# A reciprocal on one engine replaced by a guess and a polynomial on three, and edits at both ends of a long mix

## What is computed

```python
y = (A * p + E * vt) / (A * q + E)          # per row and channel; p, q carried over time
x = x + y
comb = top-2 of softmax(xn @ gate_w.T), scattered over 8 experts
moe = sum_e comb_e * (silu(xn @ Wg_e.T) * (xn @ Wu_e.T)) @ Wd_e.T
sh  = sigmoid(xn @ wsg.T) * (silu(xn @ Sg.T) * (xn @ Su.T)) @ Sd.T
out = x + moe + sh
```

## Time and profile before

| | us |
|---|---|
| median of 3 runs (lowest, highest) | 553.49 (552.86, 554.25) |
| the profiled execution | 557.75 |
| its span | 555.6 |
| PE busy | 476.0 (86%) |
| PEld busy | 317.2 (57%) |
| DVE busy | 427.5 (77%) |
| POOL busy | 339.0 (61%) |
| ACT busy | 272.7 (49%) |
| reciprocals (L1205), 64 of them | 57.4 |

### The profile page before, as it was taken

How to read it: one execution, slowest core, us unless ns; L and a number is a source line. 1 busy time by engine, 2 the same in 40 slices (tenths; PEclk the granted TensorE clock), 3 DMA queues, 4 the chain that set the end, 5 groups by cost and what they waited for, 6 DMA issues and landing times.

```text
span 555.6 us, 11206 instructions
## 1 busy us (share of the span) xinstructions
PE 476.0 (86%) x3293; PEld 317.2 (57%) x3293; DVE 427.5 (77%) x956; ACT 272.7 (49%) x531; POOL 339.0 (61%) x419
## 2 busy tenths in 40 slices
PE   0045868999999999999999979899999999999970
PEld 0034545777677677676777757555545555555530
DVE  5989999999999999999998667576656666666650
ACT  4867466286484674865836634423333333333310
POOL 5976768648858868588584651423485565555332
PEclk9999789999999999999999989999999999999995
DMA  7971111114323314241215010425486676576453
GB/s 297 411 296 40 42 35 38 59 59 143 106 59 134 97 41 166 62 170 60 87 68 175 22 51 2 116 70 102 78 152 115 120 133 118 105 134 121 67 74 38
DMA packets 25932, 59.21 MB, mean 107 GB/s; under 512 B 6314, under 2 KB 6314, under 8 KB 24338
## 3 DMA queue, kind: packets, MB, share of 16 engines
q0 software_dynamic: 9824, 20.90, 21.0%
q1 hardware_dynamic: 16050, 37.59, 19.0%
HBM read 37.83 MB, written 20.65 MB: 105 GB/s over the span
## 4 chain that ended last, share of the span: by engine, by line
PE 37%; DVE 26%; POOL 11%; issue 10%; DMA 7%; ACT 4%; SPq 1%; another core or an unknown queue 1%; POOLq 0%; ACTq 0%; DVEq 0%
PE GU L964 13%; PE GU L1003 8%; PE DN L979 7%; DMA out<-wall,cb 5%; PE DN L1019 5%; DVE wall L1205 5%; PE XT L907 3%; DVE st L1208 2%; DVE wall L1198 2%; POOL wall L463 2%; DVE wall L1191 2%; DVE th L1318 2%; ACT wall L657 2%; DVE hx L1325 2%; DVE HS L1320 1%
## 5 line engine op out<-in xcount | busy, mean ns | idle before, releaser
L1003 PE MATMUL GU<-xt,wall 128*128 128x256 f16 x1536 | 190.9, 276 | 3.1 <-DVE xt L1230 2.4
L1003 PEld LDWEIGHTS GU<-xt,wall 128*128 128x128 f16 x1536 | 150.2, 99 | 35.1 <-DVE xt L1230 2.8
L613 POOL DMA_INDIRECT out<-wall,cb x39 | 62.0, 1590 | 81.8 <-SPq L390 36.8
L1019 PE MATMUL DN<-wall,hx 128*128 128x512 f16 x384 | 95.3, 385 | 7.2 <-DVE xb L1332 3.0
L682 ACT ACTIVATE th<-GU,scl 128x256 f32<-128x256 f32 x103 | 48.7, 473 | 95.5 <-PE GU L1003 46.0
L691 ACT ACTIVATE hx<-HS 128x256 f16<-128x256 f32 x103 | 39.2, 381 | 94.7 <-PE HS L907 55.6
L1325 DVE TENSOR_TENSOR hx<-HS,hx 128x256 f16<-128x256 f32 x103 | 42.8, 415 | 50.3 <-ACT hx L691 45.2
L1019 PEld LDWEIGHTS DN<-wall,hx 128*128 128x128 f16 x384 | 36.9, 99 | 43.9 <-issue 7.0
L964 PE MATMUL GU<-wall,kb 128*128 x240 | 61.4, 379 | 0.2 <-issue 0.2
L964 PE MATMUL GU<-wall,xnb 128*128 x228 | 58.5, 379 | 1.6 <-DVE xnb L1524 1.6
L1318 DVE SCALAR_TENSOR_TENSOR th<-th,GU 128x256 f32<-128x256 f32 x103 | 41.6, 404 | 23.7 <-ACT th L682 23.7
(11 more groups left out here) (166 smaller groups left out, 804.3 us busy)
## 6 DMA issues: line engine op xcount, KB each, us to landing
wall<-wgu SPq DMA_DIRECT2D x12, 1024.0 KB, 7.7
wall<-wd SPq DMA_DIRECT2D x12, 512.0 KB, 8.6
out<-xb SPq DMA_DIRECT2D x20, 256.0 KB
xb<-x SPq DMA_DIRECT2D x16, 256.0 KB, 2.9
cb<-ctx_t SPq DMA_DIRECT2D x16, 256.0 KB
xn_rows<-xnb SPq DMA_DIRECT2D x16, 256.0 KB
xb<-xn_rows,cb POOLq DMA_INDIRECT x39
out<-wall,cb POOLq DMA_INDIRECT x39
```

What stands on the lines that cost most here:

```text
L613: pool.indirect_dma_start(out, bass.IndirectOffsetOnAxis(ap=idsa[:, j:j + 1], axis=0), ye[j % RESULTS], None, compute_op=ALU.add).then_inc ...
L1003: ins = nc.tensor.matmul(GU[n % 2][:, g * 2 * P:(g + 1) * 2 * P], gate_up(sh_base(u // 2), wp, c)[:, f:f + P], xt_pair(n // PU * 2, xp, c) ...
L1019: ins = nc.tensor.matmul(DN[a][:], hx[n % 2][:, hp * IE + a * P:hp * IE + (a + 1) * P], down(sh_base(u // 2), wp, u % 2), start=u == 0 and ...
```

## The change

For tiles 4 to 15 the reciprocals and the product go away. ScalarE makes a first guess of 1/q from the bits of q (`guess`: an exponential of the integer pattern, 128 x 512), GpSimd multiplies denominator and numerator with it (`trial`, and copies the first column), ScalarE squares the first product twice with two shifts (`correction`), and VectorE multiplies the second product with the two quadratic factors (`divide`: 4 x 127 elements per partition, twice). Tiles 0 to 3 keep the reciprocal. `both_exps` waits for the finished quotient in place of GpSimd's product. ScalarE's high parts of an odd turn stand one place earlier.

In the ramp GpSimd waits for `add_now` of tiles 1 and 3 at two places, `shared_d_lo(0)` comes ahead of `quotient(2)`, three constants are added, and `hidden(3)` goes behind the small steps. At the other end of the mix `accumulate` comes ahead of `rows_of_lists`, the list's cast, transpose and copies come earlier (`last_expert_lo` behind them), and `earlier_adds` leaves the last expert's end out, so that an unused slot waits like a slot of the last expert.

```diff
+DIV = LAG + 1
+GUESS_SCALE, GUESS_BIAS = -math.log(2) / (1 << 23), 127 * math.log(2) + math.log(2 / 2.0614756908398154)
+DIV_SCALE = 1.0002892772687446
+DIV_BIAS, DIV_ADD = (-0.691182891301668, -1.8095403018701928), (0.9041945157263527, 0.3453715725662169)
...
-CONSTS_FIRST, CONSTS, LATE_CONSTS, WKVC = 9, 17, 2, 6
+CONSTS_FIRST, CONSTS, LATE_CONSTS, WKVC = 9, 20, 2, 6
...
+                for k, value in enumerate((GUESS_BIAS, *DIV_BIAS)):
+                    link(pool.memset(divc[:, k:k + 1], value))
...
+            def trial(t):
+                pool.wait_ge(guessed, t - DIV + 1)
+                nc.gpsimd.tensor_tensor(wkv(t, 2), wkv(t, 2), wkv(t, 0), ALU.mult).then_inc(tried, 1)
+                nc.gpsimd.tensor_tensor(wkv(t, 3), wkv(t, 3), wkv(t, 0), ALU.mult).then_inc(ymul, 1)
+
+                pool.wait_ge(ymul, t + 1)
+                nc.gpsimd.tensor_scalar(chunks(wkv(t, 3))[:, :, 0:1], chunks(part(cb, t))[:, :, 0:1], 1.0, None,
+                                        ALU.mult).then_inc(y_first, 1)
+
...
+            pool.wait_ge(nd, 2)
...
             first_product(3)
             second_product(3)
+            shared_d_lo(0)
             quotient(2)
-            shared_d_lo(0)
             norm(4, 0, agg1, norm1, k_rdy)
+            pool.wait_ge(nd, 4)
             shared_d_lo(1)
...
                 if lo_e is not None:
                     expert_lo(lo_e, 2)
+                trial(i)
                 if ws_e is not None:
                     expert_lo(ws_e, 0)
                 if i + 2 < B:
...
                 if i + 1 < B:
                     first_product(i + 1)
                     second_product(i + 1)
-                quotient(i)
                 if sq_e is not None:
                     scales(sq_e + 2, sq_e)
...
                 act.wait_ge(kp1, t + 1)
-                wait_from(act, ymul, t - 1)
+                wait_from(act, y_rdy, t - 1)
...
+
+            def guess(t):
+                act.wait_ge(nd, t + 1)
+                nc.scalar.activation(wkv(t, 0), wkv(t, 2).bitcast(I32), ACT.Exp, bias=divc[:, 0:1],
+                                     scale=GUESS_SCALE).then_inc(guessed, 1)
+
+            def correction(t):
+
+                act.wait_ge(tried, t - DIV + 1)
+                nc.scalar.activation(wkv(t, 1), wkv(t, 2), ACT.Square, bias=divc[:, 1:2],
+                                     scale=DIV_SCALE).then_inc(corrected, 1)
+                nc.scalar.activation(wkv(t, 2), wkv(t, 2), ACT.Square, bias=divc[:, 2:3],
+                                     scale=DIV_SCALE).then_inc(corrected, 1)
...
                 unit_tanh(n, 0, SHARED)
                 router_out(i - 2)
+                guess(i)
                 if i == B - 1:
...
                 act_hi(i - 1)
                 if i + 2 < B:
                     first_norm(i + 2)
+                correction(i)
                 unit_hi(n + 2, 0)
+                if hi_e is not None:
+                    expert_piece(hi_e, 0)
                 unit_tanh(n + 3, 1, SHARED)
                 if hi_e is not None:
-                    expert_piece(hi_e, 0)
+                    expert_piece(hi_e, 1)
                 if ws_e is not None:
                     expert_piece(ws_e, 4)
                 unit_hi(n + 3, 1)
                 if hi_e is not None:
-                    for k in range(1, 4):
+                    for k in range(2, 4):
                         expert_piece(hi_e, k)
                 if ws_e is not None:
...
-            shared_units(B - LAG + 2, beyond={1: [lists_t], 3: [lambda: gathered_t(0, 0)]})
+            shared_units(B - LAG + 2, beyond={0: [lists_t], 3: [lambda: gathered_t(0, 0)]})
...
+
+            def divide(t):
+                dve.wait_ge(ymul, t + 1)
+                dve.wait_ge(corrected, (t - DIV) * 2 + 2)
+                later = [grid(wkv(t, r))[:, :, 1:T] for r in range(4)]
+                STT(later[3], later[1], DIV_ADD[0], later[3], ALU.add, ALU.mult).then_inc(half_div, 1)
+                dve.wait_ge(half_div, t - DIV + 1)
+                STT(later[3], later[2], DIV_ADD[1], later[3], ALU.add, ALU.mult).then_inc(y_rdy, 1)
...
             first_stats(5)
             keys(4)
-            hidden(3, 1, SHARED)
             reciprocals(3, 2, 2)
             act_lo(2)
             small_steps(1, 0)
+            hidden(3, 1, SHARED)
...
                 if i == B - 1:
                     probabilities(0, 0, PART)
-                reciprocals(i, 0, 1)
                 hidden(n + 1, 1, SHARED)
                 if i + 1 < B:
                     keys(i + 1)
-                reciprocals(i, 1, 2)
                 hidden_lo(n + 1, 1)
-                reciprocals(i, 3, 1)
                 hidden(n + 2, 0, SHARED)
                 act_lo(i - 1)
+                divide(i)
                 small_steps(i - 2, i - 3, None if sq_e is None else sq_e + 2)
...
                 dve.wait_ge(pads_rdy, 1)
                 dve.wait_ge(rt_pos, 3)
-                wait_step(TT(cmp, cmp, r_end.unsqueeze(1).to_broadcast([P, NSLOT, E]), ALU.mult))
-                wait_step(nc.vector.tensor_reduce(r_eid, cmp, AX.X, ALU.max))
+                former = cmp[:, :, 0:E - 1]
+                wait_step(TT(former, former, r_end[:, 0:E - 1].unsqueeze(1).to_broadcast([P, NSLOT, E - 1]), ALU.mult))
+                wait_step(nc.vector.tensor_reduce(r_eid, former, AX.X, ALU.max))
...
             hidden_lo(n, 0)
             small_steps(l=B - 1)
-            rows_of_lists()
             accumulate(B - 4)
             accumulate(B - 3)
+            rows_of_lists()
             hidden(n + 1, 1, SHARED)
...
             small_steps(k=E + 1)
             hidden_lo(n - 1, 1)
-            hidden(n, 0, SHARED)
             dve.wait_ge(ids_ld, 16)
             nc.vector.tensor_copy(ids_float.unsqueeze(2), ids_back.rearrange("r (p a) -> r p a", a=LW)[:, :, 0:1]
                                   ).then_inc(ids_f, 1)
+            hidden(n, 0, SHARED)
             hidden_lo(n, 0)
-            last_expert_lo(E - 2, 0)
-            last_expert_lo(E - 2, 1)
             dve.wait_ge(ids_t, 1)
             nc.vector.tensor_copy(idsi, KT[:, 0:NSLOT]).then_inc(ids_rdy, 1)
             dve.wait_ge(pads_rdy, 1)
             TT(idsa, KT[:, 0:NSLOT], pad_of, ALU.add).then_inc(ids_rdy, 1)
+            last_expert_lo(E - 2, 0)
+            last_expert_lo(E - 2, 1)
             hidden(n + 1, 1, SHARED)
             hidden_lo(n + 1, 1)
```

7 lines of the change are left out of this document (added).

## The result

| | before | after |
|---|---|---|
| median (lowest, highest), 4 runs each | 553.87 (552.86, 554.94) | 580.72 (578.91, 584.25) |
| ratio, 95% interval | | 1.0492 (1.0455 to 1.0529) |
| the profiled execution, its span | 557.75, 555.6 | 578.91, 577.1 |
| mean granted TensorE clock in it | 0.977 | 0.973 |
| busy: PE, DVE | 476.0, 427.5 | 479.7, 401.3 |

The account below looks back on a forecast made before the run. TensorE was taken as the bound, VectorE close behind, with a chain of waits setting each turn; turns +29, lists -2.8, first gather -0.5, last add -4.9, ramp 0 make +20.8 us on 553.5: 574 us, range 556 to 587.

Parts of the forecast that it names:

- The bound and the chain: Turns: norm, trial, low part, norm, first norm, squares, factors in line; even turns 17.4 to 20.5 us, odd 19.2 to 22.7.
- The signs named ahead: Turns: VectorE idle ahead of L1244, ScalarE ahead of L664, TensorE waiting 1 to 3 us; last add 0.3 us behind rows.
- Rival (a): Whole kernel: the chain has slack, VectorE decides, TensorE runs without waits; 539.6 us, chance 0.17.
- the ring: Turns: the path of waits across engines from one start of the scans to the next, forecast at 20.5 and 22.7 us.
- Rival (b): Odd turns: later scans escape GpSimd's scale steps, 2.3 us per odd turn come back; 564 us, chance 0.12.
- Contention, 0.4 us per turn: Turns: VectorE's two-input factors stretch beside GpSimd's products; 0.4 us added per turn, 10 us more in all with 1.27.
- "+2" and "+1": Forecast extra us: +2 for turns 4 and 5 together, +1 for turns 14 and 15 together.
- By these accounts all would fit: Per tile, busy time: VectorE 2.4 us less, ScalarE 1.8 more, GpSimd 1.25 more, which by itself would fit.
- Both ends: Ramp and end of the mix: lists -2.8 us, first gather -0.5, last add -4.9, ramp 0.
- the lists: End of the mix: `accumulate` moved ahead, six products done in the shade of TensorE's wait; -2.8 us (0 to -4.3).
- The ramp at 0: Start of the kernel: gains at tile 1 and a later product of tile 2 put at 0, between -2 and +3 us.
- rival (c): Turns: TensorE's stop for the quotient in odd turns lowers its clock; +6 us, 580 us, chance 0.08.

Follow-up runs that it names:

- squares_first: The changed kernel with the two squares put ahead of the first norm on ScalarE: 565.02 us, 1.0211 of the kernel before.
- ends_only: The kernel before with `accumulate` first, the list's cast, transpose and copies earlier, and the shorter waits of unused slots: 547.3 us, ratio 0.9875.
- adds_only: The kernel before with only the shorter waits of unused slots: 549.47 us, ratio 0.9945.
- the parts alone: Three runs, each with one part of the change on the kernel before: division in the turns 585.4 us, ramp 554.62 us, end edits 547.3 us.
- division_only: The changed kernel with the ramp and the end put back as before: 585.4 us, 1.0588 of the kernel before.
- high_first: The changed kernel with the squares and the high part ahead of the first norm on ScalarE: 564.51 us, 1.0241 of the kernel before.
- lows_last: The changed kernel with GpSimd's order changed to both norms and the trial, then all low parts, then the products: 581.23 us, ratio 1.051.

## Why the prediction was right in sign and 7 us short

**The bound and the chain: right.** "A turn can't be shorter than the longest path that leads from one start of the scans to the next" gave 20.5 and 22.7 us; measured 20.1 to 20.3 and 22.5. In the odd turn, counted from its scans (185.94), the trial ends after 15.5 us (forecast 15.6), the squares after 18.9 (18.7), the next scans come after 22.5. squares_first is the counterproof: with the squares out of the line, all else equal, 15.7 us come back. The signs named ahead are in the rows, two figures a little outside what was named: idle time ahead of L1244 (2.26 in turn 8, 3.66 in turn 9, forecast 1.5 to 3) and of L664 (1.12 and 2.60), TensorE's waits ahead of the result's transposes (0.67 and 3.23, forecast 1 to 3), the last add (567.50) 0.3 us behind the rows (566.41 + 0.81).

**Rival (a), VectorE decides: wrong**, as argued. VectorE's relief is real and worth nothing while the ring holds.

**Rival (b), odd turns catch up: wrong.** The scale steps collide with the scans as before, since both shift together: in turn 9 three of them take 1.02, 1.16 and 1.18 us, and before 1.04, 1.16 and 1.18.

**Contention, 0.4 us per turn: right here by luck, wrong as a price.** In the changed kernel ten of twelve first factors take 0.69 to 0.83 us: in an even turn L1244 starts at 182.18 and GpSimd's last product ends at 182.5. In turns 4 and 14 they meet (1.67 + 1.63 and 1.34 + 1.64 in place of 1.38), which is 1.9 and 1.6 us, and covers the 2.8 by which turns 4, 5, 14 and 15 exceed their "+2" and "+1". The rule of the Trainium skill's page "SBUF — State Buffer", section "Who interferes with whom", weighed in the prediction, is borne out where there is a meeting: two SBUF operands on VectorE against a reading GpSimd, and the loser waits out the pass (0.69 becomes 1.3 to 2.65, a low part being 2.13). The reciprocals, with one operand, kept their 0.93 beside the same passes. What decides is the moment; I should have asked where each GpSimd pass lies when a factor starts, in place of a mean stretch.

**"By these accounts all would fit": short.** The busy account of each engine did fit, and after the squares were moved, odd turns still took 20.7 to 21.2 us, through a norm behind a low part. An account by engine says nothing of the passes of GpSimd and VectorE that hold each other up.

**Both ends: the last add right, the lists three times too large.** The last add stands 4.9 us earlier in the profile, as forecast. For the lists the forecast took -2.8 because the six products behind the stop took 2.72 us and would be done in its shade. But 2.72 is their time at the lower clock of that one execution; the same products behind the same stop take 1.46 to 1.51 us in three other kernels, and lists and gathers together give about 1 us for 3.3; that the profile's -2.9 came near was luck. Some 1.1 and 4.9 make 6.0, against 6.2 timed in ends_only (3.8 to 10.1) and 8.2 forecast. That adds_only alone was timed at 3.0 doesn't fit and stays open.

**The ramp at 0:** +1.7 in the profile. The low part ahead of tile 2's quotient took 4.12 us, not 2.1, since it meets VectorE's reads, and TensorE waited for tiles 2 and 3:

```profile
52.14 4.12 POOL L532 TENSOR_TENSOR wall<-wall 128x1024 f16<-128x1024 f32 x1
```

```profile
59.62 1.11 PE L946 MATMUL YT<-ident,wall 128*128 128x128 f32 x4 [7.95 <-POOL wall L462]
...
82.64 1.11 PE L946 MATMUL YT<-ident,wall 128*128 128x128 f32 x4 [6.23 <-POOL wall L462]
```

**Where the 6 us between 20.8 and 26.9 lie.** By the parts alone: division 31.9 for 29, ramp 1.1 for 0, ends -6.2 for -8.2, 2.9 + 1.1 + 2.0 = 6.0, each with an interval wider than itself. For the first there is a candidate, rival (c), whose figure of 580 the median matches, though I gave it 0.08. Behind two of the four stops of 3.2 us in the changed kernel TensorE's clock is lower, in turns 7 and 11; behind those of turns 9 and 13 it isn't. Turn 7 to 8:

```profile
163.67 0.71 PE L946 MATMUL YT<-ident,wall 128*128 128x128 f32 x4 [3.24 <-DVE wall L1246]
164.18 1.49 PE L1043 MATMUL GU<-xt,wall 128*128 128x256 f16 x6
165.46 2.50 PE L1059 MATMUL DN<-wall,hx 128*128 128x512 f16 x6
```

Six products take 2.50 us in place of 1.47, and the turn 20.33 in place of 20.07. In division_only the clock is lower behind all four, and the same place gives this window and a turn of 21.52:

```profile
163.71:185.22 21.51, 20.72 (x155) 14.61 (x153) 14.72 (x41) 15.38 (x30) 11.96 (x19) 0.91 0.14 40
```

Most of it vanishes in the slack that the ring leaves to TensorE, but not all, and the runs differ by it: the four of the changed kernel have mean clocks of 0.961 to 0.973, the slowest (584.25) the lowest. That it makes up the whole 2.9 is argued, not shown.

## What to carry to other kernels

Before moving work off a busy engine, write down the ring through which one iteration hands on to the next, with the start of each link: the new work costs its full length if its input comes late in the ring, whatever the busy shares say, and an instruction that could run waits for whatever stands ahead of it in its own engine's program. Where operations move to two-operand forms on VectorE, lay them beside GpSimd's passes in time; an order that left the chain short and put low parts under the factors made turns 6 to 13 7.3 us longer. And look at the whole kernel after a reordering, not only at the stretch that it was meant for: one comparison of 16 numbers behind the last turn, caught by two low parts, took back 5 us in three of these kernels. Time a small, sure edit (the end's, here) apart from the large one, so that it isn't thrown away with it.

## What the runs showed of the hardware

- A VectorE operation too small to matter isn't when it meets GpSimd: 128x16 operations with two SBUF operands went from 0.16 to 1.5 us beside one GpSimd pass and to 4.9 when two followed each other. A conversion of 128x2 with a single SBUF operand, which I had not expected to be held up, did the same; in high_first (ns):

```profile
L1329 DVE TENSOR_SCALAR chosen<-ix x16: 164/170/1717, 63.3 to 337.0; 128x2 f32<-128x2 uint32 x16
```

The Trainium skill's page "SBUF — State Buffer", section "Who interferes with whom", allows for it: it counts `tensor_scalar` among the operations that can enter a mode that takes the shared ports. MAX8, FIND_INDEX8 and BATCH_NORM_STATS2 beside the same passes didn't stretch.

- The same stop of TensorE was followed by a lower clock in some turns and not in others. Of the four stops of 3.2 us in the changed kernel, two were followed by six products of 2.50 and 2.46 us and two by 1.47. Behind the four of 2.2 us in lows_last the transposes took 0.79, 1.11, 0.66 and 0.66 us (0.60 without a stop). So one profile doesn't price a stop: the profile of the kernel before has 2.72 us for products that take 1.46 behind the same stop in two other kernels.
